# Convolution stage: kernel-expanding matmuls over two 64-row halves of the array

## What is computed

```python
enh  = conv_dw3x3(conv1x1(x))                    # 128 channels
attn = conv1x1(h1 * h2) * attgamma + conv1x1(x)  # 16 numbers per pixel (NSET = 16)
bias = einsum('bpn,nc->bpc', attn, selfb[0])
attk = einsum('bpn,nm->bpm', attn, selfw[0])     # per pixel: 64 groups x 2 x (2 * 9) weights
# each pixel has its own 3x3 kernel: out channel i of a pair from both channels of the pair
y    = einsum('bpgij,bpgj->bpgi', attk, patches(enh)) + bias
out  = y * ga1 + enh + x
```

## Time and profile before

| | |
|---|---|
| median of three runs | 6341.05 us |
| profiled execution, its span | 6337.7 us |
| first kernel matmul of layer 1 to the last | 2158.3 to 6327.7 us |
| one band in the steady state | 65.39 us |
| TensorE / VectorE / GpSimd busy in one band | 62.43 / 62.21 / 56.95 us |

### The profile page before, as it was taken

How to read it: one execution, slowest core, us unless ns; L and a number is a source line. 1 busy time by engine, 2 the same in 40 slices (tenths; PEclk the granted TensorE clock), 3 DMA queues, 4 the chain that set the end, 5 groups by cost and what they waited for, 6 DMA issues and landing times.

```text
span 6337.7 us, 114032 instructions
## 1 busy us (share of the span) xinstructions
PE 5965.4 (94%) x37896; PEld 4228.6 (67%) x37896; DVE 5468.8 (86%) x5380; ACT 3542.2 (56%) x4544; POOL 4620.0 (73%) x1894
## 2 busy tenths in 40 slices
PE   8999999999999699999999999999999999999998
PEld 7777777777777366666666666666666666666666
DVE  6777777777776799999999999999999999999999
ACT  6777777777777444444444444444444444444443
POOL 4444444444444688888888888888888888888886
PEclk9999999999999799999999999999999999999999
DMA  2222221112221221122222212121122222112221
GB/s 80 66 66 66 66 66 64 65 64 65 66 66 56 60 68 60 61 64 63 66 63 63 63 62 64 63 66 61 60 64 63 66 63 67 60 61 64 63 66 43
DMA packets 303448, 403.66 MB, mean 64 GB/s; under 512 B 38192, under 2 KB 202736, under 8 KB 303344
## 3 DMA queue, kind: packets, MB, share of 16 engines
q1 hardware_dynamic: 303008, 402.45, 20.1%
q10 hardware_dynamic: 400, 0.69, 0.1%
HBM read 152.26 MB, written 136.31 MB: 46 GB/s over the span
## 4 chain that ended last, share of the span: by engine, by line
PE 49%; issue 9%; DVE 8%; SPq 0%; DVEq 0%; POOL 0%; DMA 0%; ACT 0%; POOLq 0%
PE ps_k L826 16%; PE ps_t L842 16%; PE ps_m L809 9%; DVE products L1055 5%; PE ps_p L795 3%; PE ps_t L859 2%; DVE products L1062 1%; PE ps_t L857 1%; PE ps_t L850 1%; PE ps_m L816 1%; DVE h_prod L1079 1%; DVE products L1021 0%; SPq L631 0%; POOL enh L753 0%; DVEq L1053 0%
## 5 line engine op out<-in xcount | busy, mean ns | idle before, releaser
L753 POOL TENSOR_TENSOR enh<-enh,tap 128x1280 f32<-128x1280 f32 (+1 forms) x1024 | 2830.2, 2764 | 164.7 <-ACT tap L972 115.8
L1055 DVE TENSOR_TENSOR products<-ps_k,enh 128x1024 f32<-128x1024 f32 x2304 | 2750.2, 1216 | 214.2 <-PE ps_k L826 187.8
L826 PE MATMUL ps_k<-att,basis 128*128 128x512 f32 x4608 | 1763.9, 464 | 195.6 <-DVE products L1055 190.7
L842 PE MATMUL ps_t<-ident,products 128*128 128x128 f32 x12288 | 1569.5, 272 | 0.0
L842 PEld LDWEIGHTS ps_t<-ident,products 128*128 128x128 f32 x12288 | 1427.1, 141 | 184.3 <-issue 0.2
L826 PEld LDWEIGHTS ps_k<-att,basis 128*128 128x128 f32 x4608 | 716.2, 190 | 1087.9 <-DVE products L1055 629.1
L254 POOL TENSOR_TENSOR hidden_lo<-hidden,hidden_hi 128x1024 fp32r<-128x1024 f32 x256 | 651.8, 2566 | 913.4 <-DVE hidden_hi L452 913.4
L972 ACT ACTIVATE tap<-e,dw 128x1280 f32<-128x1280 f32 (+1 forms) x1024 | 1245.6, 1248 | 7.6 <-POOL enh L753 7.6
L1062 DVE TENSOR_TENSOR products<-products 128x1024 f32<-128x1024 f32 x512 | 1109.4, 2167 | 0.0
L765 POOL TENSOR_TENSOR products<-products 128x1024 f32<-128x1024 f32 x256 | 614.2, 2399 | 410.5 <-DVE products L1055 410.5
L809 PE MATMUL ps_m<-xin,gT 128*32 128x512 f32 x4608 | 815.2, 610 | 6.7 <-DVE bias_att L1012 6.7
(11 more groups left out here) (108 smaller groups left out, 7590.9 us busy)
## 6 DMA issues: line engine op xcount, KB each, us to landing
xt<-in_x SPq DMA_DIRECT2D x128, 512.0 KB, 4.1
layer_out<-xo SPq DMA_DIRECT2D x128, 512.0 KB, 2.9
out<-out_sb SPq DMA_DIRECT2D x256, 256.0 KB, 2.0
xin<-layer_out SPq DMA_DIRECT2D x63, 896.0 KB, 5.5
enh<-enh SPq DMA_DIRECT2D x128, 325.0 KB, 2.6
enh<-enh SPq DMA_DIRECT2D x128, 260.0 KB, 2.4
xin<-layer_out SPq DMA_DIRECT2D x63, 384.0 KB, 6.0
att<-att_hi SPq DMA_DIRECT2D x512, 32.0 KB, 1.9
```

The source lines that it names most:

```text
L753: nc.gpsimd.tensor_tensor(own, own, tap_sb[add % TAP_BUFFERS][:, 0:hi - lo, :], ALU.add).then_inc(dw_done, 1)
L826: mm = nc.tensor.matmul(ps_k[q % 2][:, BANK * s:BANK * (s + 1)], basis[:, 2 * t + s, :], att[p][:, j, :], start=True, stop=True)
L842: mm = nc.tensor.matmul(ps_t[j % 2][:, C * r:C * (r + 1)], products[:, q % PRODUCTS, s, C * r:C * (r + 1)], ident[:, :], is_transpose=True ...
L1055: nc.vector.tensor_tensor(products[:, q % PRODUCTS, :, :].rearrange("c s (h w) -> c s h w", w=W), ps_k[q % 2][:, :].rearrange("c (s h w) - ...
```

## The change

The two kernel matmuls of a slot no longer contract over all 128 rows. The 16 attention rows are laid down eight times without gaps: rows 16(2c) carry `att_hi` and rows 16(2c + 1) `att_lo`, for c = 0..3. Rows 0 to 63 hold the own channel's basis, rows 64 to 127 the partner's, each with a high and a low part. Matmul s = 0 uses rows 0 to 63, s = 1 rows 64 to 127, in different banks. `basis` shrinks to 10 slots. The DMAs of `attention_rows` go from 16 to 32 a band, and the counts waited for from 256 to 512 for two bands. In the preparation the memsets of `sw_raw` and `att` go and the ACT queue gets 4 more DMAs. The 36 multiplications that build the basis stay, over 64 partitions each.

```diff
-    SLOTS = 2 * TAPS + 1
+    SLOTS = TAPS + 1
+    K_ROWS = C // 2
...
-                    for block_row, src in ((0, att_hi), (1, att_hi), (2, att_lo), (3, att_lo)):
-                        if block_row == 2:
+                    for part, src in enumerate((att_hi, att_lo)):
+                        if part == 1:
                             sp.wait_ge(att_lo_ready, m + 1)
                         for j in range(CHUNKS):
-                            sp.dma_start(att[p][32 * block_row:32 * block_row + NSET, j, :].bitcast(FP32),
-                                         src[32 * j:32 * j + NSET, :].bitcast(FP32)).then_inc(att_in[p], 16)
+                            for copy in range(4):
+                                r = NSET * (2 * copy + part)
+                                sp.dma_start(att[p][r:r + NSET, j, :].bitcast(FP32),
+                                             src[32 * j:32 * j + NSET, :].bitcast(FP32)).then_inc(att_in[p], 16)
...
                     for s in range(2):
-                        mm = nc.tensor.matmul(ps_k[q % 2][:, BANK * s:BANK * (s + 1)], basis[:, 2 * t + s, :], att[p][:, j, :],
+                        rows = slice(K_ROWS * s, K_ROWS * (s + 1))
+                        mm = nc.tensor.matmul(ps_k[q % 2][:, BANK * s:BANK * (s + 1)], basis[rows, t, :], att[p][rows, j, :],
                                               start=True, stop=True)
...
-                                pe.wait_ge(att_in[b], rounds(m, b, 256) + 256)
+                                pe.wait_ge(att_in[b], rounds(m, b, 512) + 512)
...
-                for j in range(4):
-                    act.dma_start(sw_raw[32 * j:32 * j + NSET, :], selfw[0]).then_inc(loaded["basis"], 16)
-                    act.dma_start(sb_raw[32 * j:32 * j + NSET, :], selfb[0]).then_inc(loaded["basis"], 16)
+                for j in range(8):
+                    act.dma_start(sw_raw[NSET * j:NSET * (j + 1), :], selfw[0]).then_inc(loaded["basis"], 16)
+                    if j < 4:
+                        act.dma_start(sb_raw[NSET * j:NSET * (j + 1), :], selfb[0]).then_inc(loaded["basis"], 16)
...
-                        act.wait_ge(att_in[1 - p], rounds(m - 1, 1 - p, 256) + 256)
+                        act.wait_ge(att_in[1 - p], rounds(m - 1, 1 - p, 512) + 512)
...
-                nc.vector.memset(sb_raw[:, :], 0.0)
-                nc.vector.memset(sw_raw, 0.0).then_inc(zeroed_basis, 1)
-                for p in range(2):
-                    nc.vector.memset(att[p][:, :, :].bitcast(FP32), 0.0)
+                nc.vector.memset(sb_raw[:, :], 0.0).then_inc(zeroed_basis, 1)
...
-                            nc.vector.tensor_tensor(basis_full[:, 2 * t + s, :].rearrange("n (g i) -> n g i", i=2)[:, :, i:i + 1],
-                                                    by_group[:, :, col:col + 1], ga[:, :, i:i + 1], ALU.mult)
+                            rows = slice(K_ROWS * s, K_ROWS * (s + 1))
+                            nc.vector.tensor_tensor(basis_full[rows, t, :].rearrange("n (g i) -> n g i", i=2)[:, :, i:i + 1],
+                                                    by_group[rows, :, col:col + 1], ga[rows, :, i:i + 1], ALU.mult)
```

More of the change, by code:

```diff
@@ L606, in convolve @@
         stored = [sem(f"chunk_stored{j}") for j in range(CHUNKS)]
-        LOADS, BASIS_LOADS = {"pointwise": 4, "grouped": 2 + CHUNKS * 6}, 1 + 4 * 2
+        LOADS, BASIS_LOADS = {"pointwise": 4, "grouped": 2 + CHUNKS * 6}, 1 + 8 + 4
         ring_memory = products[:, :, :, :].rearrange("c a s n -> c (a s n)")
```

## The result

The changed kernel takes 6695.98 us (median of 4 runs, 6692.9 to 6701.12) against 6341.44 us for the kernel before beside it: ratio 1.0557, 95% interval 1.0545 to 1.057. It is slower by about 355 us. The forecast was 6738 us, range 6500 to 6930. The profiled execution has a span of 6691.1 us.

What follows compares the result with a forecast made beforehand. It took neither TensorE nor VectorE alone to bound the convolution stage. Per band +4.4 (copies), +1.0 (array) and +0.8 us (clock) over 63 bands, plus 7 us at the start, gave 6738 us, range 6500 to 6930.

Steps and rivals of the forecast that it cites:

- The copies bound: SP's 32 attention copies take 21.7 us against 17.26 us of cover; TensorE waits at slot 34, +4.4 us a band.
- The rest of the band does not shrink: Slot 34 to the next first copy keeps its 48.13 us, so the wait adds fully to the band.
- The array: Two 64-row kernel matmuls replace two 128-row ones: +1.0 us a band, whole interval -1.95 to +5.5.
- The middle case: Kernel matmuls side by side but paying the change of division: 0.67 us a pair against 0.47, +0.6 to +3.6 a band.
- high case: Kernel matmuls one after the other, changing division twice a slot: 9.2 us a band, 6.9 in the 48.13 us part.
- The clock: TensorE's clock halves for a while behind each band's wait: +0.8 us a band, ends 0 and 1.6.
- The start: Preparation and first band: uncovered copies cost 10.1 us, smaller basis work saves 3.2; +6.9 us, once.
- The sum: Convolution stage: +6.2 us a band over 63 bands plus 7 at the start, +398 us in all.
- Rival A: Convolution stage: copies bound, TensorE's gain shrinks the rest to 46.2 us; 6505 to 6555 us, partly 6620; chance 0.22.
- Rival B: Kernel matmuls not side by side and paying the change of division; band +9 to +13, 6920 to 7160 us; chance 0.13.
- rival C: Faster: SP issues copies under 0.49 us each, hidden, and TensorE's gain reaches VectorE's floor; 6190 us; chance 0.05.

Runs made afterwards that it cites:

- the copies alone: Kernel before, full-row matmuls, each copy issued a second time into unused rows with zero basis, 32 copies a band: 6538.63 us, ratio 1.031.
- Experiments 1, 3 and 8: Changed kernel with waits by chunk: 6351.41 us; with only 16 copies a band: 6357.01 us; with the att_lo copies issued from ScalarE's queue: 6358.64 us.
- experiment 7: Changed kernel with waits by chunk, but both matmuls of a slot use rows 0 to 63: 6757.17 us, ratio 1.0659.
- experiment 6: Kernel before with each copy issued twice, plus two 512-column filler matmuls before the wait: 6528.79 us, ratio 1.0298.
- experiment 5: Changed kernel with three 512-column filler matmuls (12 instructions) before the wait for the copies: 6569.34 us, ratio 1.0369.

## Why the prediction was right, point by point

**The copies bound.** Right to the tenth. Forecast: 19.6 us to the last issue and 2.08 to land, 21.7 us from first copy to first kernel pair; measured 21.66, with the copies alone 21.67 and with fillers 21.65. The first part of the band grew by the 4.4 us of the forecast. The idle time in it was put at 3 to 4.5 us and measured 3.57: TensorE is busy for 18.09 us there instead of 17.26. Experiments 1, 3 and 8 each remove the wait in another way (order of the copies, their number, a second queue) and each brings back 337 to 345 of the 355 us.

**The rest of the band does not shrink.** Here the sum had an error of size: "48.13 us from slot 34 to the next first copy" was taken over unchanged. At a clock of 1.00 it is 46.00 us with the copies alone, so the copies cost 4.4 - 2.1 = 2.3 us a band and not 4.4. The rows show who uses the wait. GpSimd was busy for 46.34 of the 48.13 us and for 10.61 in the first part; with the wait the first part has 14.39 us of it and the second 40.70, so it works on while TensorE stands. VectorE's merges, too, take 16.3 us in the band shown instead of 17.6, and 15.0 with fillers. That these two are what shortens the second part is likely. No run tested it.

**The array.** Forecast +1.0, "about the middle of -1.95 and +3.6". The middle case, side by side but with the change of division, is the true one: experiment 7 and the 3 ns between the starts show the first, the 1.02 us transposes the second. Its price was too high, 0.67 us for a pair with its way out; measured are 0.42 + (1.02 - 0.88) = 0.56 against 0.47. And slots behind the grouped convolution gain 0.22 us instead of staying even. In sum 24 x 0.10 - 12 x 0.22, about -0.2 us a band by these prices; TensorE's busy time with the waits by chunk is 62.48 against 62.43, and the kernel comes out 10 us slower (ratio 1.0015). Behind the single wait the row tiles cost more, 0.8 us a band (experiment 6). So +1.0 was near, but it was a choice between two wide ends, and its upper end of +5.5 for the unknown stands beside a high case worked out to 3.9 to 6.9: that it came close is in part luck. The page "TensorEngine Tiling (Array Packing)" of the Trainium skill, Key Properties, has both halves of this, draining at a change of mode and parallel work of tiles; with 0.14 us on the transposes behind a pair and 0.24 us saved in it, the trace agrees with both for row tiles now.

**The clock.** Forecast +0.8 a band, ends 0 and 1.6; experiment 5 puts it at 127 us in all, 127 / 63 = 2.0 a band, and at 2.3 over the bands without a gap. The mechanism was right and the term mis-sized, from above its upper end. Two things were wrong in it. The time at the lower level was taken as 3.2 us a band, from one wait of 2.72 us; it is some 5 us. And the halving for work that falls "where VectorE is the slower one" had no ground: the work just behind the wait is the grouped convolution and kernel pairs that TensorE paces, 0.80 for 0.49 and 1.86 for 1.01 in the chain.

**The start.** +14.1 us instead of +7: the first kernel pair comes at 2172.43 instead of 2158.30. The copies gave what was computed, 10.1, and the smaller basis saves its 3 us. But the multiplications that build the basis begin at 2113.76 instead of 2106.55: VectorE is released from its loads 4.7 us later, and the first nine instructions behind take 2.5 us longer. In all runs with the changed preparation SP's first copy is 3.8 to 5.5 us late, with the copies alone 1.6. The forecast had these loads cost nothing; which of them it is was not looked for.

**The sum.** Over the last 35 whole bands of each trace a band takes 65.47 us before (SP's first copies at 3904.69 and 6196.10) and 70.81 after, +5.3 where +6.2 was forecast: about +2.3 for the copies, +0.8 for the array and +2.3 for the clock, against 4.4, 1.0 and 0.8. The misses of the first and the last term nearly cancel, and that is luck. In all 63 x 5.3 + 14 = 348 of the measured 353 us between the two spans, against 398 forecast. Rival A, a second part that shrinks to VectorE's floor, is true in its direction once the clock is taken out (46.79 where the floor was put at 46.2), though not through TensorE: the copies alone, with full rows, show 46.00. Its total, at most 6620, was missed, since it had the clock at 0 to 0.8. Rival B's first condition is excluded by experiment 7, and rival C by the copies' spacing, 0.63 us instead of under 0.49.

## What to carry to other kernels

Count every DMA that a layout costs on the queue that issues it, and set issues x price + landing against the stretch that covers them; a layout that saves matmul rows is not free if it doubles small copies. A wait should ask for the part that the next instruction reads: with waits by chunk the same 32 copies are free here. A wait on TensorE can cost more than its length: here 3.57 us idle went with 5.3 us a band, 2.3 of them by the clock. When computing such a wait, take the stretch at the lower clock from several waits and not from one, and ask which other engine works on meanwhile and gives part of the wait back.

## What the runs showed of the hardware that was not expected

A change of the array's division shows as 0.14 us on the eight transposes behind a kernel pair, while the pair itself, with 64 rows in each half, costs 0.42 us; two full-row matmuls cost 0.47, and two matmuls in the same 64 rows 0.66. Behind a visit of the grouped convolution the row-tiled pair costs 0.43 to 0.45, where the full-row pair had 0.65.

Idle time of 2.06 us before a kernel pair already went with a fall of the clock: the full-row copies-only kernel has a pair of 1.21 us behind it. In the next band 2.12 us of idle time went with none, the pair took 0.73 us, and the second part was 0.94 us shorter. With waits of about 3.5 us the changed kernel has a fall in each band, and in sum it loses at least 127 us by it.

Fifty-six short instructions more in TensorE's loop over bands brought 50 gaps, such as 1.66 and 1.84 us, and 286 packets of instruction loads in place of 24; twelve instructions for nearly the same work brought 42 packets and two gaps, 3.07 and 2.82 us.
